# Four-layer graph network on one core: the scatter of the cells in loops over spans, with index and payload in fixed tiles

## The reference

```python
edge_index = jnp.stack([src, dst])
deg = jnp.maximum(segment_sum(ones, dst), 1.0)
h = relu(layernorm(x)); x = x + L0(h, src, dst, deg)      # h @ Ws.T + (mean of neighbours) @ Wn.T, layernorm
h = relu(layernorm(x)); x = x + L1(h, edge_index, edge_weight)   # two GCN convolutions, rows to length 1
h = relu(layernorm(x)); x = x + L2(h, edge_index, edge_attr_128) # message MLP over edges, sum, GRU, batch norm
h = relu(layernorm(x)); x = x + L3(h, edge_weight1, src, dst)    # weighted sum of neighbours @ W.T
```

## Time and profile before

| | us |
|---|---|
| median of 3 runs | 1461.65 (1454.98 to 1465.86) |
| the profiled execution | 1465.06 |
| its span | 1463.3 |
| busy: PE, DVE, POOL, ACT | 1204.0, 1014.9, 691.7, 571.7 |
| POOL busy with L711, the cells' scatter | 168.3, 168 instructions |
| first and last column of it start at | 42.8 and 296.9 |

### The profile page before, as it was taken

How to read it: one execution, slowest core, us unless ns; L and a number is a source line. 1 busy time by engine, 2 the same in 40 slices (tenths; PEclk the granted TensorE clock), 3 DMA queues, 4 the chain that set the end, 5 groups by cost and what they waited for, 6 DMA issues and landing times.

```text
span 1463.3 us, 20037 instructions
## 1 busy us (share of the span) xinstructions
PE 1204.0 (82%) x4298; PEld 748.8 (51%) x4298; DVE 1014.9 (69%) x2113; ACT 571.7 (39%) x1461; POOL 691.7 (47%) x760
## 2 busy tenths in 40 slices
PE   4410056579799999999999889999999999998998
PEld 1310023244344444455787655444444478887787
DVE  9750017645499999985237868888888889888543
ACT  0200011121377777022201128888887753334210
POOL 0577735710288888067667726666666500000000
PEclk9655568789899999999999999999999999999899
DMA  8811001511400000733422467777777600002220
GB/s 335 307 59 59 2 30 37 187 58 72 155 21 24 25 19 11 291 100 114 141 84 88 144 212 231 228 215 230 217 224 222 163 1 1 0 1 74 82 90 35
DMA packets 87258, 167.89 MB, mean 115 GB/s; under 512 B 16124, under 2 KB 44670, under 8 KB 84644
## 3 DMA queue, kind: packets, MB, share of 16 engines
q1 hardware_dynamic: 59588, 102.69, 20.8%
q0 software_dynamic: 25472, 59.97, 13.5%
q10 hardware_dynamic: 2144, 4.59, 1.0%
HBM read 115.96 MB, written 51.23 MB: 114 GB/s over the span
## 4 chain that ended last, share of the span: by engine, by line
PE 64%; DVE 12%; another core or an unknown queue 8%; issue 6%; DMA 3%; DVEq 2%; ACT 2%; POOL 2%; SPq 1%; ACTq 0%; POOLq 0%
PE pb L1328 10%; PE pb L1103 6%; PE pb L1228 6%; PE pb L1220 5%; PE pb L1423 5%; PE pb L1193 4%; PE pb L1396 4%; PE pb L1398 4%; PE pb L1397 4%; PE pb L1171 3%; PE pb L1342 3%; PE pb L1344 2%; PE pb L1345 2%; PE pb L1321 2%
## 5 line engine op out<-in xcount | busy, mean ns | idle before, releaser
L711 POOL DMA_INDIRECT cell_rows<-pay,idx x168 | 168.3, 1002 | 125.8 <-DVE idx L1569 74.5
L745 POOL DMA_INDIRECT dst_rows<-ering,gidx x168 | 172.4, 1026 | 100.8 <-issue 90.2
L1328 PE MATMUL pb<-arena 128*128 128x512 f32 x368 | 191.0, 602 | 13.0 <-ACT arena L970 12.5
L1113 PE MATMUL pb<-ident,arena 128*128 128x128 f32 x164 | 34.2, 382 | 132.6 <-issue 52.1
L799 POOL DMA_INDIRECT arena<-p_rows,arena x96 | 99.5, 1036 | 78.0 <-issue 26.9
L1897 DVE TENSOR_TENSOR arena<-pb,arena 128x512 f32<-128x512 f32 x184 | 122.1, 681 | 7.1 <-DMA arena<-p_rows,arena 3.7
L799 POOL DMA_INDIRECT arena<-p_rows,ws x88 | 92.6, 1052 | 50.7 <-issue 25.9
L1904 DVE SCALAR_TENSOR_TENSOR low<-arena,high 128x512 fp32r<-128x512 f32 x138 | 95.0, 688 | 29.2 <-ACT high L977 21.5
L855 ACT ACTIVATE arena<-iota,free 128x128 f32<-128x128 f32 x266 | 92.2, 394 | 53.3 <-PE pb L1193 39.5
L1540 DVE TENSOR_TENSOR arena<-pb,arena 128x505 f32<-128x505 f32 (+1 forms) x34 | 23.0, 677 | 126.3 <-remote 116.2
L813 ACT COPY ws<-pb 128x512 f32<-128x512 f32 x40 | 22.7, 589 | 224.5 <-remote 109.7
(11 more groups left out here) (329 smaller groups left out, 2663.0 us busy)
## 6 DMA issues: line engine op xcount, KB each, us to landing
dst_rows<-arena SPq DMA_DIRECT2D x6, 2046.0 KB, 17.5
ering<-in_edge_attr_dram SPq DMA_DIRECT2D x41, 256.0 KB
arena<-adj SPq DMA_DIRECT2D x10, 640.0 KB, 4.0
arena<-dst_rows SPq DMA_DIRECT2D x24, 264.0 KB
arena<-wt_gru SPq DMA_DIRECT2D x48, 128.0 KB
ws<-dst_rows SPq DMA_DIRECT2D x22, 264.0 KB
arena<-in_x_dram SPq DMA_DIRECT2D x18, 256.0 KB
arena<-in_L_gnn_W_hh_dram SPq DMA_DIRECT2D x3, 1024.0 KB
```

Of the source, the lines that this page charges most:

```text
L711: nc.gpsimd.indirect_dma_start(cell_rows[:, :], bass.IndirectOffsetOnAxis(idx1[:, j:j + 1], 0), pay1[:, j], None).then_inc(c_scattered[spa ...
L745: nc.gpsimd.indirect_dma_start(dst_rows[:, :], bass.IndirectOffsetOnAxis(gidx[:, k:k + 1], 0), ering[:, k, :], None).then_inc(e_scattered[ ...
L1328: nc.tensor.matmul(e_bank(k)[:], erowT[:, k % 4], w1e_sb, start=True, stop=True).then_inc(edge_mm, 1)
```

## The change

The scatter of a batch becomes a prologue, a loop over pairs of spans, and an end. Ahead of each span, POOL copies its five columns of payload to `cring`, a ring of two spans in `tiles[:, 3]`, and its five columns of indices to `gidx`; the second copy raises `cells_indexed`, and the span's DMAs wait for it. The DMAs read only the fixed tiles, with the span's parity `a`. The copies for a span stand behind the DMAs of the span before it, behind the wait for the span that used the same half of the ring. The batches, the number of columns and the semaphores of landing are the same. The additions of DVE to the matrices stay in halves, as they are.

```diff
+        cring = tiles[:, 3, 0:2 * SPAN * 4].rearrange("p (a c w) -> p a c w", a=2, c=SPAN)
...
-            def scatter_whole(span):
-
-                at_least(pool, c_scattered[span % 2], 16 * SPAN * (span // 2))
+            def index_span(i, a, n=SPAN):
+
+                at_least(pool, c_scattered[a], 16 * SPAN * i)
                 passed()
-                for j in range(SPAN * span, min(SPAN * span + SPAN, J)):
-                    nc.gpsimd.indirect_dma_start(cell_rows[:, :], bass.IndirectOffsetOnAxis(idx1[:, j:j + 1], 0),
-                                                 pay1[:, j], None).then_inc(c_scattered[span % 2], 16)
-
+                c = bass.ds(SPAN * (2 * i + a), n)
+                nc.gpsimd.tensor_copy(cring[:, a, 0:n], pay1[:, c, :])
+                nc.gpsimd.tensor_copy(gidx[:, SPAN * a:SPAN * a + n], idx1[:, c]).then_inc(cells_indexed, 1)
+
+            def scatter_span(i, a, prepare_next, n=SPAN):
+
+                pool.wait_ge(cells_indexed, 2 * i + a + 1)
+                passed()
+                for k in range(n):
+                    nc.gpsimd.indirect_dma_start(cell_rows[:, :], bass.IndirectOffsetOnAxis(gidx[:, SPAN * a + k:SPAN * a + k + 1], 0),
+                                                 cring[:, a, k], None).then_inc(c_scattered[a], 16)
+                if prepare_next:
+                    prepare_next()
+
+            rest = J - SPAN * (SPANS - 1)
             for n in range(len(BATCHES) - 1):
+                first, last = BATCHES[n] // 2, BATCHES[n + 1] // 2 - 1
+                final = n == len(BATCHES) - 2
                 pool.wait_ge(order_ready[0], n + 1)
                 passed()
-                for span in range(BATCHES[n], BATCHES[n + 1]):
-                    scatter_whole(span)
+                index_span(first, 0)
+                if last > first:
+                    with pool.Fori(first, last) as i:
+                        scatter_span(i, 0, lambda: index_span(i, 1))
+                        scatter_span(i, 1, lambda: index_span(i + 1, 0))
+                scatter_span(last, 0, lambda: index_span(last, 1, rest if final else SPAN))
+                scatter_span(last, 1, None, rest if final else SPAN)
```

## The result

The changed kernel takes **1370.51 us** (median of 4 runs, 1370.14 to 1371.79); the kernel before, beside it, 1461.49 (1454.98 to 1465.86). The ratio is 0.938, with a 95% interval of 0.935 to 0.942. One thing has to stand ahead of its reading. Of the five sets of runs that I have (the kernels of a set run one after another on one chip), four found the kernel before at 1460 to 1473 us, and one at 1327. The ratio was measured in one of the four, and again in another (0.935). For the fifth, see "The set in which the news was prompt".

The account below looks back on a forecast made before the run. Late news of PE's work during POOL's cell scatter was taken to bound the kernel. With it prompt, POOL's scatter ends the stage, the copy moves from 388.0 to 297: 91 less, taken as 88, 1465 - 88 = 1377, median 1375 us; range 1364 to 1493.

Parts of the forecast that it names:

- The bottleneck: During POOL's cell scatter, news of finished PE work reaches ACT and DVE 10 to 28 us late; about 100 us lost.
- Part 1: POOL's own cost in the cell scatter: a pause adding 0.83 us per span, +28 us over 34 spans.
- Part 2: Waits on `c_scattered` in POOL's cell scatter, now guarding the two ring halves: cost zero.
- Part 3: Branches of POOL's new loop, 12 iterations: priced at nothing, from above 0.8 us each, 10 us.
- Part 4: POOL's copies beside DVE in the cell scatter: 5 us added, as last-batch columns averaged 1.06 us, not 0.97.
- The sum: Whole kernel if the pauses let PE's news through: 1465 - 88 = 1377, median 1375 us; chance 0.41.
- PE's part: PE's work ending at 241.9 would end near 140, and the stores near 271 us.
- The landing: After POOL's last cell column at 291: landing 2 us, then load 4 us, so the copy starts at 297.
- the two ends meeting: POOL's scatter end and the stores' end meeting close together: 88 us gained in place of 91.
- A: Rival: PE's news stays late, from the rate of 16-byte scatters, and pauses only cost 26 us; 1488 us, chance 0.39.
- D: Rival: copies don't part POOL's columns; cost below 28 us, time near 1462; chance 0.11 shared with another rival.

Follow-up runs that it names:

- e11: Kernel before plus, every fifth column, a 128x512 POOL product and a wait for the one a group back; 1357.50 us, beside 1327.31 for the kernel before.
- e1: Changed kernel with its POOL loops written out as straight line, same copies and waits; 1373.17 us, ratio 0.941 to the kernel before.
- e4: Kernel before with 528-byte rows in place of 16, written to a scratch tensor; 1464.8 us in one run.
- e2: Kernel before plus a one-word POOL memset and a wait for it after every fifth column; 1388.96 us, ratio 0.949.
- e8: Kernel before plus a one-word POOL memset and a wait for it after every tenth column; 1460.31 us, ratio 1.000.
- e3: Kernel before plus one POOL memset every fifth column, not waited for until the last column is out; 1462.51 us, ratio 1.001.
- e5: Kernel before plus seven one-word POOL memsets after every fifth column, with no wait inside the line; 1431.85 us, ratio 0.979.
- e6: Kernel before plus two one-word POOL memsets ahead of each column, with no wait inside the line; 1446.10 us, ratio 0.990.
- e7: Kernel before plus a one-word POOL memset and a wait for it after every fourth column; 1372.50 us, ratio 0.938.
- e10: Kernel before plus, every fifth column, a POOL memset and a wait for the one a group back; 1328.27 us, beside 1327.31 for the kernel before.

## Why the prediction was right, point by point

**The bottleneck.** Right in the sets with late news: news, not work. POOL's 87 us of slack were real, and the change spends them. The copies come 0.8 us apart, not 11.2; DVE's indices for the last batch were there before POOL asked (no idle time ahead of it).

**Part 1, POOL's price.** +0.83 us a span was the forecast; 7.21 - 6.38 = 0.83 is what the timeline shows. e11 shows the other half of it, that each us of this kind falls on the end once the scatter sets it.

**Part 2.** The waits on `c_scattered` ended no idle time in the table of waits: zero, as priced. **Part 3.** Zero is right: e1 without branches is no faster, 1373.17 against 1370.51 us. But the reading behind it was wrong: behind the branch of L745's loop stand the two copies, and the first column after them had 0.82 or 0.86 us of idle time in each group (the earlier trace rows show one), though only every second group has a branch ahead of it; no column with 0.30 follows a branch. Nor does that disagree with the Trainium skill ("Runtime: NRT & Kernel Launch", section "Instruction fetch mechanics"), which charges a taken branch only where its target isn't in the two pages at hand; no run here shows that cost. And "nothing on the end" doesn't fit the forecast's own sum, in which POOL ends the stage. **Part 4.** POOL was to go from 59.3 to 291 with 5 us for columns beside DVE. It went from 59.06 to 290.04 + 0.96 = 291.0. The 5 us are right in size and wrong in place: the mean of 1.06 us hid two columns of 1.82 and 3.68 us, at 234.89 and 237.01, beside DVE's two long instructions. These came at 122 to 129 us in the changed kernel, and the last 70 columns took 0.972 us each.

**The sum.** PE's part was sized too long: its work that ended at 241.9 ended at 130.2 (forecast 140), and the stores were out at 257.9 (271). That cost nothing, because POOL was later, as forecast. The landing took 1.2 us (291.0 to SP's load at 292.21), not 2. I had taken 88 us and not 91 for the two ends meeting; they lie 34 us apart, so the 3 us were needless. The copy at 388.02 came at 295.74 (297). Together: 1370.5 against 1375. That it is so close holds some luck: these small errors cancel in part, and the large question, whether 0.83 us in 7.2 was rest enough, was put at 0.41 against 0.39, with a range, 1364 to 1493, that held both answers.

**The rivals.** A (the lateness stays) had 0.39 and named the rate of 16-byte scatters; e4 is as late with rows of 528 bytes. But A was nearer than the result looks: e2, with 0.2 us less a span, kept half of the lateness, and e8, with half the pauses, nearly all of it. The 0.83 us were just enough, and in the repeat 12 us of `remote` were back. In D's sense, e3 is a change whose instruction doesn't part the columns, and it did nothing.

**What the prediction didn't see.** It names the pause as what helps. The runs show gains without any wait (e5, e6) and none with a pause per ten columns (e8), so "a pause lets the news through" is too simple. Pauses close enough together do it (e7, and the changed kernel); whether by the distance that they make, by how it is dealt out, or by the wait is open, and so is why POOL's line holds up PE's news at all. And it took the late news for a property of the kernel. It depends on the set: one of five had none, and there even the low end of the range, 1364, lies 37 us above the time of the kernel before.

## What to carry to other kernels

Where consumers wait `remote` for work whose end the trace shows 10 us earlier, look at what another engine issues without a break meanwhile, and try short pauses, a few instructions apart, before changing the work itself. Find out first whether the wait is there in every set: by the estimate above the cure costs 26 us of the engine that ends the stage, and it pays only while the news is late. An instruction put in to make distance must not fit into gaps that are there already; the trace tells (seven memsets took 0.29 us).

## What the runs showed of the hardware that I had not expected

- **The same kernel, 1327 or 1461 us.** On one chip, within some ten minutes, the kernel before took 1460.72, then 1327.31, then 1473.13 us as a median; within each set it keeps to 11 us. The traces of the late sets also hold far fewer records of DMA landings: 6,444 in that of before against 12,889 in that of e10, for the same transfers. Within the late sets they go with the news: 6,259 to 6,555 where over 100 us are `remote`, 6,680 to 7,696 in the four traces with 12 us or less. Whether the lack of records and the lateness have one cause, and whether an execution that isn't recorded shows the lateness, is open.
- **The gather stage is longer in the late sets too.** From the first to the last of SP's 48 loads of `wt_gru`, which keep step with the gathers, it is 253.2 to 253.6 us in the three traces of the prompt set and 264.9 to 275.7 in the eleven of the late sets, whatever the kernel. Two loads from the timelines of SP's queue, the changed kernel and then e11, with 37 loads from one to the other in each:

```profile
797.41 0.35 SPq L641 DMA_DIRECT2D arena<-wt_gru  x1
...
1034.40 0.34 SPq L641 DMA_DIRECT2D arena<-wt_gru  x1
```
```profile
800.32 0.35 SPq L640 DMA_DIRECT2D arena<-wt_gru  x1
...
1021.17 0.34 SPq L640 DMA_DIRECT2D arena<-wt_gru  x1
```

  That is 237.0 us against 220.9. The profile has hardly a `remote` entry there (none in the changed kernel), so that this is late news as well is a guess. The two traces of before and e10 differ by 139.3 us of span: 117 are there when the cells are loaded (383.94 against 267.01), 14 come in this stage. So in a late set the changed kernel still loses some 16 us, in a stage that it doesn't touch; a version that spaces the gathers was not tried.
- **The relation is steep.** From a pause every fifth column to one every fourth (e2 to e7, 1.38 to 1.41 us a column) the `remote` waits fell from 119 us to 9.
- **A column's issue is long beside DVE's scan.** With DVE's scan of 128x1848 bf16, 4.0 us long, one column took 3.68 us before and 3.87 us in the changed kernel in place of 0.97, and both ended 0.8 us behind the scan.
